# The last three sequences of a language-model tower: a tail written out by hand, with denominators and expert weights spread by TensorE

## What is computed

```python
h = tok(x)                                       # position + nesting + segment rows, times W
q, k, v = layernorm(h) @ qkv_w.T + qkv_b         # 8 heads of 16
attn = softmax(q @ k.T / 4)                      # per head, 512 x 512
h = h + (attn @ v) @ out_w.T + out_b
g = softmax(xn @ gate_w.T) - sigmoid(xn @ thr_w.T) / 4     # xn = layernorm(h), 4 experts
w = where(g >= 0, g, 0); w = w / (sum(w) or 1)
h = h + sum_e w[e] * fc2[e] @ (loB[e] @ (loA[e] @ relu(fc1[e] @ xn)))
```

## Time and profile before

| | us |
|---|---|
| median of 3 runs (1123.06 to 1123.34) | 1123.27 |
| the profiled execution's own time | 1124.57 |
| its span, first to last instruction | 1122.8 |
| TensorE busy | 1040.9 |
| VectorE busy | 923.4 |
| ScalarE busy | 819.2 |
| GpSimd busy | 721.5 |
| mean granted TensorE clock, as a share of full speed | 0.957 |

### The profile page before, as it was taken

How to read it: one execution, slowest core, us unless ns; L and a number is a source line. 1 busy time by engine, 2 the same in 40 slices (tenths; PEclk the granted TensorE clock), 3 DMA queues, 4 the chain that set the end, 5 groups by cost and what they waited for, 6 DMA issues and landing times.

```text
span 1122.8 us, 20355 instructions
## 1 busy us (share of the span) xinstructions
PE 1040.9 (93%) x6158; PEld 408.6 (36%) x6158; DVE 923.4 (82%) x2410; ACT 819.2 (73%) x1610; POOL 721.5 (64%) x716
## 2 busy tenths in 40 slices
PE   5378899999999999999999999999999999999955
PEld 3012234433434434333334334333433443333322
DVE  7498888889988898888988889888998889888111
ACT  2317787878877888788877788787877788777731
POOL 1865667787666776677666677678666777622332
PEclk8558999999999999999999999999999999999986
DMA  2554545555555455555554455655555445541110
GB/s 69 149 134 94 130 108 142 129 128 132 137 128 125 121 130 130 138 121 135 137 129 122 126 123 129 142 124 128 136 137 129 124 122 124 127 103 44 51 49 30
DMA packets 93530, 132.43 MB, mean 118 GB/s; under 512 B 18205, under 2 KB 69918, under 8 KB 87398
## 3 DMA queue, kind: packets, MB, share of 16 engines
q1 hardware_dynamic: 91872, 129.54, 47.9%
q10 hardware_dynamic: 1550, 1.59, 0.5%
HBM read 89.20 MB, written 35.01 MB: 111 GB/s over the span
## 4 chain that ended last, share of the span: by engine, by line
PE 66%; DVE 17%; DMA 7%; ACT 4%; issue 3%; POOL 1%; SPq 1%; POOLq 0%; ACTq 0%
PE pv L751 17%; PE mix L764 16%; PE sc L738 13%; DVE negmax L1039 9%; PE mix L818 8%; DMA den_dram<-ctx_sb 3%; PE mix L801 3%; DVE bn L1029 2%; PE mix L823 2%; ACT probs L600 2%; DVE h L1065 2%; PE mix L839 2%; DMA den<-den_dram 2%; PE mix L783 1%; PE mix L776 1%
## 5 line engine op out<-in xcount | busy, mean ns | idle before, releaser
L1039 DVE TENSOR_REDUCE negmax<-mix 128x1 f32<-128x512 f32 x1024 | 648.7, 678 | 61.4 <-PE mix L764 61.0
L600 ACT ACTIVATE probs<-sc 128x512 f32<-128x512 f32 x1024 | 556.9, 601 | 116.2 <-PE sc L738 112.3
L738 PE MATMUL sc<-qstk,kstk 120*128 120x512 bf16 x1024 | 363.2, 381 | 5.3 <-ACT probs L600 4.6
L764 PE MATMUL mix<-kstk,qstk 96*128 96x512 bf16 x1024 | 330.3, 393 | 25.7 <-DMA kstk<-stack_dram 7.6
L751 PE MATMUL pv<-probs,vals 128*32 128x512 f32 x2048 | 244.8, 595 | 0.0
L531 POOL TENSOR_TENSOR ctxh<-ctx_sb,rdenb 128x512 f32<-128x512 f32 x64 | 80.8, 1267 | 183.7 <-DMA rdenb<-rden_dram 101.8
L764 PEld LDWEIGHTS mix<-kstk,qstk 96*128 96x128 bf16 x1024 | 89.4, 98 | 266.7 <-issue 82.2
L738 PEld LDWEIGHTS sc<-qstk,kstk 120*128 120x128 bf16 x1024 | 99.8, 98 | 106.3 <-ACT probs L600 33.3
L818 PE MATMUL mix<-xn2T,fc1T_sb 128*128 128x512 f32 x256 | 137.7, 620 | 0.7 <-ACT hid L659 0.7
L509 POOL TENSOR_TENSOR qk<-qk,rstdb 128x512 f32<-128x512 f32 x64 | 81.1, 1269 | 67.6 <-DMA rstdb<-rstd_dram 67.6
L751 PEld LDWEIGHTS pv<-probs,vals 128*32 128x32 f32 x2048 | 59.1, 109 | 117.4 <-issue 100.1
(11 more groups left out here) (142 smaller groups left out, 1114.6 us busy)
## 6 DMA issues: line engine op xcount, KB each, us to landing
stack_dram<-pieces SPq DMA_DIRECT2D x192, 128.0 KB
rdenb<-rden_dram SPq DMA_DIRECT2D x64, 256.0 KB
qstk<-stack_dram SPq DMA_DIRECT2D x31, 384.0 KB, 6.5
kstk<-stack_dram SPq DMA_DIRECT2D x31, 384.0 KB, 8.6
rstdb<-rstd_dram SPq DMA_DIRECT2D x32, 256.0 KB, 3.4
wrow<-w_dram SPq DMA_DIRECT2D x32, 256.0 KB
out<-out_sb SPq DMA_DIRECT2D x32, 256.0 KB, 4.9
qstk<-stack_dram SPq DMA_DIRECT2D x31, 256.0 KB, 6.8
```

Source lines behind the costliest of these rows:

```text
L600: act.activation(probs[:, c % 8, i % 2], sc[:, i % RING], ACT.Exp).then_inc(s_exp, 1)
L738: pe.matmul(sc[:, i % RING, :], kstk[0:KROWS, u, h, j * P:(j + 1) * P], qstk[0:KROWS, u, h, :], start=True, stop=True).then_inc(s_score, 1)
L764: pe.matmul(max_bank(m), qstk[0:STK, u, h, j * P:(j + 1) * P], kstk[0:STK, u, h, :], start=True, stop=True).then_inc(s_mxmm, 1)
L1039: dve.tensor_reduce(negmax[:, m // NT, m % NT:m % NT + 1], max_bank(m), AX.X, ALU.max, negate=True).then_inc(s_max, 1)
```

## The change

The loop `steps` now ends with step 31, and each engine gets a function `last_sequences` in its place. Sequences 29, 30 and 31 are called third, second and last there. No instruction of steps up to 31 is changed, but for the store of the denominators of sequence 31's first half, which is left out. What differs in the tail:

- TensorE runs the last two value products of sequence 31 first.
- The denominators of sequence 31 don't go through DRAM. TensorE multiplies the context by columns of the identity (`turn_den`), which puts the denominators of 128 tokens on partitions; VectorE inverts them (128x16), copies each one 16 times (`rdwide`, 128x512), and TensorE's products with the identity (`spread_den`) turn that into the broadcast tile, in PSUM. VectorE does the two products and the sum of the normalisation, where GpSimd did them.
- The expert weights of sequences 30 and 31 don't go through DRAM: the last gate product writes each weight 32 times (`wwide`, 128x512), four products with the identity (`spread_weights`) turn it, and VectorE copies it into `wrow`.
- Centring and scaling of sequences 30 and 31 move from GpSimd to VectorE; GpSimd keeps only the inverse deviation.
- The output's copy on ScalarE and sum on GpSimd become one sum on VectorE, straight from PSUM, for all three.
- `LAST` gives the products of the tail PSUM banks of their own (banks 4 to 6 are those of the score ring, 7 that of the values). The residual of sequence 31 lies in `h_sb` and its output in `ctxh`.

```diff
+LAST = {
+    ("fc1_3", -3): 0, ("low", -3): 2, ("out", -3): 3,
+    ("project", -2): 1, ("xn2T", -2): 0, ("gates", -2): 1, ("turn_gates", -2): 2, ("fc1_0", -2): 0, ("fc1_1", -2): 1,
...
-            for t in range(-5, NSEQ + 3):
+            for t in range(-5, NSEQ):
                 step(t, t % U)
...
+            def turn_den(g):
+                b = NSEQ - 1
+                upto(pe, s_ctx, b, 2, g + 1)
+                row = (HC, 0)[g]
+                for j in range(NT):
+                    mm = pe.matmul(den_bank(g)[:, 4 * j:4 * j + 4], ctx_sb[:, b % U % 2, g, j * P:(j + 1) * P],
+                                   id32[:, row:P:Q], start=True, stop=True)
+                mm.then_inc(s_denT, 1)
+
+            def spread_den(g):
+                pe.wait_ge(s_rdT, 2 * g + 3)
+                for j in range(NT):
+                    mm = pe.matmul(sc[:, 1 + g, j * P:(j + 1) * P],
+                                   rdwide[:, g, j * P:(j + 1) * P],
+                                   id32[:], start=True, stop=True)
+                mm.then_inc(s_rdb, 1)
+
+            def spread_weights(b):
+                upto(pe, s_gate, b, 13)
+                for j in range(NT):
+                    mm = pe.matmul(aux("weights", NT, b)[:, j, :], qk32[:, 0, j * P:(j + 1) * P],
+                                   id32[:], start=True, stop=True)
+                mm.then_inc(s_wTmm, 1)
...
+                turn(second, "xn2T", xn2, s_xn2, 1, s_xn2Tmm)
+                upto(pe, s_h2, second)
+                gates(second)
+                project(last)
+                upto(pe, s_low, third)
+                turn_gates(second)
+                experts_out(third)
...
+            def invert_last(g):
+                dve.wait_ge(s_denT, g + 1)
+                dve.wait_ge(s_rdT, 1)
+                dve.reciprocal(rdT[:, g, :, :, g],
+                               den_bank(g)[:, 0:16].rearrange("p (j q) -> p j q", j=NT)).then_inc(s_rdT, 1)
+                dve.wait_ge(s_rdT, 2 * g + 2)
+                dve.tensor_copy(rdwide[:, g, :].rearrange("p (n c) -> p n c", c=HC),
+                                rstdb[:, 32 * g:32 * g + 32].unsqueeze(2).broadcast_to([P, 32, HC])).then_inc(s_rdT, 1)
+
+            def normalise_half(g):
+                b = NSEQ - 1
+                dve.wait_ge(s_rdb, g + 1)
+                dve.tensor_tensor(ctxh[:, g, :], sc[:, 1 + g], ctx_sb[:, b % U % 2, g, :], ALU.mult).then_inc(s_ctxh, 1)
...
+            def finish(b):
+                upto(dve, s_outmm, b)
+                if b < NSEQ - 1:
+                    upto(dve, s_store, b - 1, 16)
+                dve.tensor_tensor(out_of(b), aux("out", NT, b), h2_of(b), ALU.add).then_inc(s_out, 1)
```

More of the change, by code:

```diff
@@ L99 @@
 ]
+LAST = {
+    ("fc1_3", -3): 0, ("low", -3): 2, ("out", -3): 3,
+    ("project", -2): 1, ("xn2T", -2): 0, ("gates", -2): 1, ("turn_gates", -2): 2, ("fc1_0", -2): 0, ("fc1_1", -2): 1,
+    ("fc1_2", -2): 5, ("fc1_3", -2): 6, ("weights", -2): 2, ("low", -2): 0, ("out", -2): 3,
+    ("project", -1): 7, ("xn2T", -1): 4, ("gates", -1): 7, ("turn_gates", -1): 1, ("fc1_0", -1): 4, ("fc1_1", -1): 5,
+    ("fc1_2", -1): 6, ("fc1_3", -1): 7, ("weights", -1): 2, ("low", -1): 0, ("out", -1): 1,
+}
 EPS = 1e-5
@@ L447, in _ @@
             steps(sp, step)
+            for b in range(NSEQ - 3, NSEQ):
+                store_out(b)
             nc.disable_value_cache = False
@@ L838, in experts_out @@
                 for j in range(NT):
-                    mm = pe.matmul(aux("out")[:, j, :], low[:, j * P:(j + 1) * P], exp_w[:], start=True, stop=True)
+                    mm = pe.matmul(aux("out", NT, b)[:, j, :], low[:, j * P:(j + 1) * P], exp_w[:], start=True, stop=True)
                 mm.then_inc(s_outmm, 1)
@@ new lines, in spread_weights, with last_sequences @@
+            def spread_weights(b):
[4 more added lines that the diff above has]
+                mm.then_inc(s_wTmm, 1)
+            def last_sequences():
+                third, second, last = NSEQ - 3, NSEQ - 2, NSEQ - 1
+                for jj in range(2):
+                    values(last, 3, jj, last % U)
+                turn_den(0)
+                upto(pe, s_gate, third, 13, 3)
+                project(second)
+                upto(pe, s_hid, third, NE, 3)
+                turn_den(1)
+                spread_den(0)
+                fc1(third, 3)
+                spread_den(1)
+                upto(pe, s_wT, third)
+                low_rank(third)
+                turn(second, "xn2T", xn2, s_xn2, 1, s_xn2Tmm)
[5 more added lines that the diff above has]
+                experts_out(third)
+                for e in range(NE):
+                    fc1(second, e)
+                turn(last, "xn2T", xn2, s_xn2, 1, s_xn2Tmm)
+                spread_weights(second)
+                low_rank(second)
+                gates(last)
+                turn_gates(last)
+                for e in range(NE):
+                    fc1(last, e)
+                upto(pe, s_out, third)
+                experts_out(second)
+                spread_weights(last)
+                low_rank(last)
+                experts_out(last)
```

132 lines of the change are left out of this document (111 added, 21 removed).

## The result

| | before | after |
|---|---|---|
| median | 1123.3 (4 runs, 1123.06 to 1125.09) | **1110.51** (4 runs, 1106.54 to 1111.39) |
| ratio, 95% interval | | 0.9873, 0.9857 to 0.989 |
| profiled execution: time; span | 1124.57; 1122.8 | 1110.2; 1107.6 |
| mean granted clock | 0.957 | 0.966 |

Faster, by 12.8 us between the medians, where 12.9 was forecast. That the two agree is partly luck, as the steps will show.

A forecast was written before the change was run, and what follows sets the result against it. TensorE bounds the steps up to 31, so only the 51.0 us tail, with its DRAM waits, can gain; nine steps sum to 38.1 us, 12.9 less, giving 1111.7 us profiled, 1110.4 median; range 1107.0 to 1116.5.

The forecast's parts named there:

- Step 1: TensorE from the tail's start: values, two `turn_den` groups at 1.09 us each and a projection; 5.13 us, to 1076.92.
- Step 2: VectorE and GpSimd: reciprocal, copy 16 times over, statistics, power and scaling of sequence 30; 4.3 us, to 1081.2.
- step 4: VectorE: gate arithmetic of 30, then residual, statistics, power and scaling of 31; 7.2 us, to 1091.8; TensorE idle 4.3.
- I charge nothing for the new neighbourhood: GpSimd's power beside VectorE's centring priced without contention; by the skill's rule the sum would be some 1.2 us higher.
- 1.94 for four `fc1`: TensorE beside VectorE's gate arithmetic of 30: four `fc1` priced at 1.94 us, done at about 1087.7, then idle.
- half clock to the end: Rival: TensorE's clock stays at half to the end of the tail; adds 5.5 us, time 1115.9; chance 0.18.
- Step 5: TensorE and ScalarE, turn of 31 to turn of its gates, four products at half clock; 6.8 us, to 1098.6.
- never lost: Rival: TensorE's clock never falls in the tail; takes off 2.7 us, time 1107.7; chance 0.12.
- The fall in step 3: Rival: the clock falls already while TensorE waits for VectorE in step 2 or 3, stays down; time 1118.0; chance 0.08.
- step 3: TensorE and ScalarE: turn, copy and gate logits of 30, projection of 31, turn of the gates; 3.4 us, to 1084.6.
- Step 6: VectorE: gate arithmetic of 31 and wide weights, four `fc1` and output of 30 beside it; 3.2 us, to 1101.8.
- Step 7: `spread_weights` of 31, VectorE's copy, finish of 30 (0.7 us on the path) and weighting; 3.4 us, to 1105.2.

The follow-up runs named there:

- e4: Changed kernel with the centring of 30 behind the first normalising product and that of 31 behind the finish of 29: median 1106.52 us, tail 35.4.
- e6: Changed kernel with 2.5 unused identity products of 512 columns in TensorE's idle time behind the fourth expert of 30: median 1108.87 us, tail 36.3.
- e8: Changed kernel with e4's exchange, two filling products of 512 columns and e7's reordering together: median 1108.91 us, tail 34.8.
- e5: Changed kernel run once more, unaltered: median 1111.3 us, tail 36.8.
- e7: Changed kernel with the first `fc1` of 31 ahead of its gates' turn, and the finish of 30 behind the weighting of 31: median 1108.54 us, tail 37.1.
- e9: Kernel before, with last values first and the projection of 31 ahead of the weights' turn and third expert of 30: median 1122.06 us, tail 51.4.
- e2: Changed kernel with the expert weights of sequences 30 and 31 sent through DRAM again: median 1115.23 us, tail 43.9.
- e3: Changed kernel with the denominators of 31 sent through DRAM again, lists fitted to that: median 1112.92 us, tail 42.0.
- e1: Kernel before, with only the last two value products of 31 and the copy of their context put first: median 1122.75 us, tail 51.5.
- e11: Changed kernel with e4's exchange and e7's reordering, without filling products: median 1108.32 us, tail 36.5.

## Why the prediction was right, and where its sum was not

Ends of the steps, in times of the trace after:

| step | foretold | measured | length foretold, measured |
|---|---|---|---|
| 1 | 1076.9 | 1076.4 | 5.1, 4.6 |
| 2 | 1081.2 | 1080.9 | 4.3, 4.5 |
| 3 | 1084.6 | 1084.05 | 3.4, 3.1 |
| 4 | 1091.8 | 1090.96 | 7.2, 6.9 |
| 5 | 1098.6 | 1095.9 | 6.8, 4.9 |
| 6 | 1101.8 | 1100.0 | 3.2, 4.1 |
| 7 | 1105.2 | 1103.04 | 3.4, 3.0 |
| 8 | 1107.2 | 1104.96 | 2.0, 1.9 |
| 9 | 1109.9 | 1107.6 | 2.7, 2.6 |

The path was the foretold one at every step but the sixth. Both trips through DRAM left it, and the runs that put them back, with the lists fitted to them, cost 4.4 and 6.2 us. The span came out 2.3 us below the forecast for the profiled execution, and its time 1.5 below (1110.2, forecast 1111.7), since it lies 2.6 us above the span and not 1.8 as before. That the median hit the forecast to 0.1 us is luck: the start of the tail alone moves by more between executions.

- **Step 1.** `turn_den` was priced at the projection's 1.09; the groups stand 0.91 and 0.81 apart. Near the upper end, as chosen.
- **Step 2, and step 4 again.** "I charge nothing for the new neighbourhood" was wrong. The setup's rows showed the power beside a VectorE product and nothing of the small sum ahead of it, which is what met the centring: 0.64 us instead of 0.20, on the path both times. The Trainium skill ("SBUF — State Buffer", Who interferes with whom) calls the port pair that VectorE and GpSimd share an exclusive lock, and says that a VectorE instruction with two SBUF inputs contends for it with GpSimd's reads. For the sum the trace agrees: it ends at 1079.09, just behind the centring's 1079.03. For the power it does not: in e4 the centring runs beside it, and they take 0.69 and 1.02 us as they do alone. My reading of the rule, a power put back by 0.6, was close to the 0.44 measured, but by another instruction; so the sign that I had set for it, a power over 1.05 us, could not show it. My ground for setting the rule aside, small operands, was no ground: the sum has the same 128x4.
- **Step 4.** The gate arithmetic, residual, statistics and wide weights took 4.0 us and not 4.5, since more of them fits in the exponential's wait. The failing term is "1.94 for four `fc1`". The row holds x4 instructions, and an `fc1` product is two of them (256 in the page before, for 4 experts of 32 sequences): 1.94 us is two products. Four take 3.6, and the idle time "4.3 us" is 2.7. The rival of the half clock to the end has the same misreading: one product took 1.91 us at half clock (before, at 1094.47), so its four with the output come to some 9.5 us by my estimate and not to 5.8, and its time to about 1119.5 us, above the range.
- **Step 5.** The mechanism held, half clock behind that idle time and full clock before the work ran out. I had let the half clock last for all products; it ended some 3.5 us after it began, inside the low-rank product (1.13 us, not 1.94). That, and the gates of 0.39 for 0.8, is the 1.9 us. Of the rivals, "never lost" came in e4, e6 and e8, each a kernel changed further, and "half clock to the end" in none. The fall in step 3 came in the kernel itself, in e5, but the clock came back 3.5 us later; that it had stayed up behind 1.4 us ahead of 1078.71 was no ground against it.
- **Step 6.** "Four `fc1` and the output of 30 are beside it" fell with the same misreading: they take 4.3 us, the gate arithmetic 3.1, and TensorE's list was the bound, by 1.0 us. e7 took 0.6 of it away.
- **Step 7.** The finish of 30 cost 0.2 us and not 0.7, since TensorE's low-rank product was still running beside it (1.20 us from the start of the copy to the weighting, and 1.02 in e7 without it).

So there are three errors of size: 1.9 us too much for the clock, 0.9 too little for contention and 0.9 too little for `fc1`. They cancel to 0.1. The 2.3 us are the sum of small terms, all priced too high: 0.5 in step 1, 0.2 and 0.7 in steps 2 and 4 beside the contention, 0.3 in step 3, 0.4 in step 7 and 0.2 in the last two.

## What to carry to other kernels

When two trips through DRAM stand one behind the other in a tail, and the engines' lists are fixed, starting the first one earlier may bring next to nothing (in e9 4.1 us for the projection and 1.5 for the tail); look for what waits next in the same list before you price it. With the lists fitted to it, a tail that keeps one trip still has most of the gain: 9.0 us in e2 and 10.9 in e3, of 15.3. Count instructions, not products, in a row of the timeline. Before you charge nothing for a new neighbour, look at every instruction of the other engine that it meets, the smallest too, and move the one with two SBUF sources a place further.

## What the runs showed of the hardware

- A GpSimd sum of 128x4 took 0.64 us when it started behind a VectorE instruction with two SBUF sources, and 0.20 beside one with a PSUM source (after, e4). GpSimd's power of the same size took 1.01 to 1.02 beside either. Why the one is held up and the other not stays open.
- The other way round, single VectorE instructions of 128x4 and 128x16 took 0.90 to 1.25 us beside GpSimd's products of 128x512, where they take 0.16 to 0.18 alone (e1, e9); some of their neighbours (a reciprocal at 0.20, a TENSOR_REDUCE at 0.17) were not held up.
- Streaming 4 columns was hardly cheaper than streaming 128: `turn_den` lasted 1.05 and 0.95 us for eight instructions, an output product of 128 columns 1.06, and the eight weight loads of each took 0.97.
- The length of one idle time did not settle whether TensorE's clock fell: 2.24 us kept it in e4 and lost it in e11; 2.68 lost it in after; 1.42 (before) and 1.56 (e5) kept it; 0.88 and 0.77 shortly after one another lost it in e5, and the same two kept it in after. Once down, it came back after 3 to 3.5 us of work without a gap in after, e5 and e11. What else decides stays open.
